# Layer norm's last step moved to ScalarE, middle parts made by a copy, and the attention loop written out

## The chip, the cores and the metric

The kernel runs on one core of a Trainium2 chip. The metric is the time on the device, in microseconds, of one execution. Engines: TensorE (PE; PEld are its weight loads), VectorE (DVE), ScalarE (ACT), GpSimd (POOL), and SyncE (SP), which only issues transfers here.

## The reference, cut to what matters

```python
# x: (32, 256, 128), 16 heads of 8
qkv = (x @ W_qkv.T + b_qkv).reshape(B, T, H, 3 * hs)
q, k, v = qkv[..., :hs], qkv[..., hs:2*hs], qkv[..., 2*hs:]
att = softmax(einsum('bthd,bshd->bhts', q, k) / sqrt(hs))
y = einsum('bhts,bshd->bthd', att, v).reshape(B, T, C) @ W_out.T + b_out
x = layernorm(x + y)                  # (r - mean) / sqrt(var + 1e-5)
# mixture of 8 experts, top 2 by sigmoid scores + bias, and a shared one
out = layernorm(x + shared(x) + sum(score * expert(score * x)))
```

## The kernel before

The work has two stages. **Attention** goes over 32 batches of 256 rows. It is a software pipeline over slots: slot s does a different step for each of nine batches. `Slot` (L165) names them: `load` is batch s+5, `proj` s+4 (keys and queries), `stack` s+3 (values, and the parts loaded back), `maxi` s+2 (scores for the row maxima), `neg` s+1, `soft` s (scores again, exp, values), `tail` s-1 (sums, division), `norm` s-2 (output product, residual, layer norm), `gated` s-3 (gate logits). Slots run from -4 to 34. `slots` (L188) writes out -4 to 2, runs 3 to 26 as a loop of six passes over four slots on each engine, and writes out the rest. In the loop, what a wait compares with depends on the pass and is worked out in registers. **The expert stage** follows: 16 groups of 512 rows, nine experts each, on all engines; its own loop is not touched.

The order within a slot is written out by hand, head by head (h = 0 to 15), with constants that say after which head a small step comes. ScalarE does one exp per head (L565, 128x512, the softmax numerator) and between them `attT`, `v_aug`, `kf`, `qf`, `attc`, `x1T_new` (`ACT_K` = 2 and so on, L174). VectorE does one reduction per head (L1008, the row maximum), and at heads 1, 2, 4: `res` (L1020), its statistics, mean and variance `mv` and `var_eps`. TensorE does four score products a head (L703, L716), the value products (L731), and small products between heads: output and key (L793, L800), values and query (L813, L817), transposes (L833, L849, L865, L871), and the gate (L840). Scores go through three PSUM banks each, so TensorE waits for the exp or the reduction of two to four heads ago. All these are in-order queues.

GpSimd (L430) does per slot: the maxima in two parts (L441, L443), `x_bo` (L457), and queries and keys split into three bf16 parts. For keys: part 0 is `kf` rounded (L463), `rk` = kf - part 0 (L465), part 1 = kf - part 0 rounded (L476), part 2 = rk - part 1 (L484); the same for queries (L485 to L490). Between them come the power that gives `rstd` (L470), two TENSOR_SCALAR that make `x1_new` from `res` (L479), and last the copy of `x1T_new` (L499). SP stores the parts to DRAM when they are done, loads them back as stacks a slot later, and stores `x1_new` (L363). TensorE transposes `x1_new` after heads 12 and 13 (L865).

In the last slots no batch is left to project, later none to take maxima of, and VectorE does the routing of the first 6144 rows between the statistics and `var_eps` of slots 30 and 31 (L959 to L976).

Of the kernel before, what the change touches and what calls it, by code (L numbers as in the profile page):

```python
# [14 lines left out]
P = 128  # L15
# [34 lines left out]
def attention_moe_layer(nc, x, xT, wqT, wkT, wvT, bq, bk, bv, woT, bo, gateT, ebias, rank, w1T, w3T, w2T, out):  # L50
# [19 lines left out]
    with ExitStack() as ctx:  # L70
# [20 lines left out]
        w_hi, w_lo = ([sb(f"{part}_{n}", [P, NE, P], F32R) for n in ("w1", "w3", "w2")] for part in ("hi", "lo"))  # L91
        ident, ident_bf = sb("ident", [P, P]), sb("ident_bf", [P, P], BF16)
        used_first = sb("used_first", [P, P])
        minus_half, ones = sb("minus_half", [P, GT]), sb("ones", [P, NT, 2, PAIRS])

        x1T = sb("x1T", [P, N])
        logits = sb("logits", [P, TILES, E])
# [18 lines left out]
        x_bo = sb("x_bo", [P, NT, C])  # L116
        res = sb("res", [P, NT, C])
        stats, mv = sb("stats", [P, NT, 6]), sb("mv", [P, NT, 2])
        var_eps, rstd = sb("var_eps", [P, NT]), sb("rstd", [P, NT])
        x1_new, x1T_new = sb("x1_new", [P, NT, C]), sb("x1T_new", [P, T])  # L120

        banks = [ctx.enter_context(nc.psum_tensor(f"bank{n}", [P, 512], F32)) for n in range(8)]
# [23 lines left out]
        tok_T, recip_set, att_norm = sem("tok_T"), sem("recip_set"), sem("att_norm")  # L146
        back_T, attc_set = sem("back_T"), sem("attc_set")
        y_mm, xbo_set, res_set = sem("y_mm"), sem("xbo_set"), sem("res_set")
        stats_set, mv_set, eps_set, rstd_set = sem("stats_set"), sem("mv_set"), sem("eps_set"), sem("rstd_set")
        x1_set, x1_kept, x1_T, x1T_set, x1T_kept = (sem(n) for n in ("x1_set", "x1_kept", "x1_T", "x1T_set", "x1T_kept"))  # L150
        gate_mm, logits_set = sem("gate_mm"), sem("logits_set")

# [18 lines left out]

        PE_YK, PE_VQ, PE_TOK, PE_BACK = 0, 2, 4, 6
        DVE_RES, DVE_STATS, DVE_AGGR, DVE_TOK = 1, 2, 4, 9
        ACT_K, ACT_ATT, ACT_V, ACT_Q, ACT_ATTC, ACT_X1T = 2, 4, 5, 6, 13, 14  # L174

# [7 lines left out]
        ACT_ROUTE = 4  # L183
        assert EARLY // NT <= B - 7

        FIRST, LOOPS = 3, (B - 8) // RING

        def slots(engine, body):  # L188

            for s in range(-4, FIRST):  # L190
                body(Slot(0, s))
            with engine.Fori(0, LOOPS) as i:
                for s in range(FIRST, FIRST + RING):
                    body(Slot(i, s))
            for s in range(FIRST + RING * LOOPS, B + 3):
                body(Slot(0, s))


# [213 lines left out]
        def _(pool):  # L412
# [2 lines left out]
            pool.affine_select(out=ident[:], in_=ident[:], compare_op=ALU.not_equal, fill=1.0, base=0,  # L415
                               pattern=[[-1, P]], channel_multiplier=1).then_inc(consts_set, 1)
            pool.memset(minus_half[:], -0.5).then_inc(consts_set, 1)
            pool.memset(ones[:], 1.0).then_inc(consts_set, 1)

            pool.wait_ge(consts_set, 4)  # L420
            pool.tensor_copy(ident_bf[:], ident[:]).then_inc(consts_set, 1)
            columns = ident[:].rearrange("p (g w) -> p g w", w=32)
            pool.tensor_copy(used_first[:, 0:4 * W].rearrange("p (g w) -> p g w", w=W), columns[:, :, 0:W]).then_inc(consts_set, 1)
# [6 lines left out]
            def slot(t):  # L430
# [31 lines left out]
                if p.live:  # L462
                    pool.tensor_copy(k_split[:, 0, :], kf[:]).then_inc(split_step, 1)  # L463
                    pool.wait_ge(split_step, p.count(8, 1))
                    pool.tensor_tensor(rk[:], kf[:], k_split[:, 0, :], ALU.subtract).then_inc(split_step, 1)  # L465
                b = t.norm
                if b.live:

                    pool.wait_ge(eps_set, b.count(1, 1))
                    pool.tensor_tensor(rstd[:], var_eps[:], minus_half[:, 0:NT], ALU.pow).then_inc(rstd_set, 1)  # L470
                    pool.wait_ge(rstd_set, b.count(1, 1))
                    if b.later(1):
                        pool.wait_ge(x1_T, b.count(1, 0))
                        pool.wait_ge(x1_kept, b.count(16, 0))
                if p.live:
                    pool.tensor_tensor(k_split[:, 1, :], kf[:], k_split[:, 0, :], ALU.subtract).then_inc(split_step, 1)  # L476
                if b.live:
                    for i in range(NT):
                        pool.tensor_scalar(x1_new[:, i, :], res[:, i, :], mv[:, i, 0:1], rstd[:, i:i + 1],  # L479
                                           ALU.subtract, ALU.mult).then_inc(x1_set, 1)  # L480
                if p.live:
                    pool.wait_ge(split_step, p.count(8, 3))
                    pool.wait_ge(qk_f, p.count(2, 2))
                    pool.tensor_tensor(k_split[:, 2, :], rk[:], k_split[:, 1, :], ALU.subtract).then_inc(split_step, 1)  # L484
                    pool.tensor_copy(q_split[:, 0, :], qf[:]).then_inc(split_step, 1)  # L485
                    pool.wait_ge(split_step, p.count(8, 5))
                    pool.tensor_tensor(rq[:], qf[:], q_split[:, 0, :], ALU.subtract).then_inc(split_step, 1)
                    pool.tensor_tensor(q_split[:, 1, :], qf[:], q_split[:, 0, :], ALU.subtract).then_inc(split_step, 1)
                    pool.wait_ge(split_step, p.count(8, 7))
                    pool.tensor_tensor(q_split[:, 2, :], rq[:], q_split[:, 1, :], ALU.subtract).then_inc(split_step, 1)  # L490

                    if p.c == RING and not p.looped:

                        for m in range(3):
                            pool.wait_ge(w_hi_set, m + 1)
                            pool.tensor_tensor(w_lo[m][:], w_stage[m], w_hi[m][:], ALU.subtract).then_inc(w_lo_set, 1)
# [39 lines left out]
        def _(act_e):  # L536
# [15 lines left out]
            def slot(t):  # L552
# [6 lines left out]
                for h in range(H):  # L559
# [17 lines left out]
                    if b.live and h == ACT_ATTC:  # L577
# [4 lines left out]
                            act_e.wait_ge(y_mm, b.count(1, 0))  # L582
                        nc.scalar.activation(attc[:], right, ACT.Identity, bias=bv_sb[:, 0:1]).then_inc(attc_set, 1)
                    b = t.norm
                    if b.live and h == ACT_X1T:
                        if t.tail.live:
                            act_e.wait_ge(back_T, t.tail.count(1, 1))
                        else:
                            act_e.wait_ge(x1_T, b.count(1, 1))
                        if b.later(1):  # L590
                            act_e.wait_ge(gate_mm, b.count(1, 0))
                            act_e.wait_ge(x1T_kept, b.count(1, 0))
                        nc.scalar.activation(x1T_new[:], left, ACT.Copy).then_inc(x1T_set, 1)
# [15 lines left out]
                    if b.live and h == ACT_K:  # L609

                        if b.c == 0 and not b.looped:
                            act_e.wait_ge(w_in, 16 * 4)
                            nc.scalar.activation(bqs[:], bq_sb[:], ACT.Copy, scale=SCALE).then_inc(bqs_set, 1)
                            act_e.wait_ge(bqs_set, 1)
                        act_e.wait_ge(k_mm, b.count(1, 1))
                        if t.norm.live:
                            act_e.wait_ge(res_set, t.norm.count(1, 1))
                        if b.later(1):
                            act_e.wait_ge(split_step, b.count(8, -5))
                        nc.scalar.activation(kf[:], right, ACT.Identity, bias=bk_sb[:, 0:1]).then_inc(qk_f, 1)  # L620
                    if b.live and h == ACT_Q:

                        act_e.wait_ge(q_mm, b.count(1, 1))
                        if b.later(1):
                            act_e.wait_ge(split_step, b.count(8, -1))
                        nc.scalar.activation(qf[:], right, ACT.Identity, bias=bqs[:, 0:1], scale=SCALE).then_inc(qk_f, 1)
                        if b.c == 0 and not b.looped:
                            load_constants()
# [64 lines left out]
        def _(pe):  # L693
# [63 lines left out]
            def slot(t):  # L757
# [11 lines left out]
                for p in range(PAIRS):  # L769
# [73 lines left out]
                    if b.live and p == PE_TOK:  # L843

                        pe.wait_ge(max_lo_set, b.count(1, 1))
                        if b.c == 0 and not b.looped:
                            pe.wait_ge(consts_set, 7)
# [363 lines left out]
```

## Time and profile before

| | |
|---|---|
| Median of 3 runs | 840.85 us (838.94 to 841.08) |
| Profiled execution | 841.11 us, span 839.3 us |
| Mean granted TensorE clock | 0.985 of full speed |
| Busy share of the span | TensorE 91%, VectorE 85%, ScalarE 66%, GpSimd 63% |
| Chain that ended last | TensorE 57%, issue 11%, GpSimd 10%, VectorE 9%, DMA 8%, ScalarE 2% |

Times in the rows count from the start of the span. Busy shares over the whole span average stages that have different limits, so the stretches have to be looked at one by one. A stretch of the chain called "issue" is time in which an engine waited for nothing that the profile shows.

### The profile page before, as it was taken

How to read it: one execution, taken by the hardware profiler on the slowest of the kernel's cores; microseconds unless marked ns; L12 is line 12 of the kernel's file. 1: busy time of each engine (PE TensorE's matmuls, PEld its weight loads, DVE VectorE, ACT ScalarE, POOL GpSimd, SP SyncE). 2: the span in 40 equal slices, each digit the busy share in tenths (PEclk: the TensorE clock that was granted, in tenths of full speed). 3: DMA queues.
4: the chain of work that ended last, by engine and by line, in shares of the span. 5: the costliest groups of instructions: out<-in, count | busy, mean ns of one | idle time of the engine just before them, and what ended most of it. 6: DMA issues, size and time to landing. Idle time of an engine off the chain costs nothing.

```text
span 839.3 us, 21651 instructions
## 1 busy us (share of the span) xinstructions
PE 761.5 (91%) x6228; PEld 471.5 (56%) x6228; DVE 709.6 (85%) x1430; ACT 557.7 (66%) x1128; POOL 528.8 (63%) x686
## 2 busy tenths in 40 slices
PE   1698999999999999999996889999999999999994
PEld 0244555555555555555544666666666666666662
DVE  5577999999999999999984788888888788888885
ACT  1147888888888888888884566655555655665651
POOL 3446766766766776676434466667666766676664
PEclk9998999999999999999999899999999999999997
DMA  5643656565565656555412724334343444444440
GB/s 157 167 118 106 169 170 169 141 186 152 159 162 168 156 149 181 153 149 163 114 35 75 180 80 109 103 102 108 103 120 110 125 125 125 125 125 124 113 90 25
DMA packets 201642, 108.83 MB, mean 130 GB/s; under 512 B 10496, under 2 KB 201088, under 8 KB 201600
## 3 DMA queue, kind: packets, MB, share of 16 engines
q1 hardware_dynamic: 200048, 105.88, 47.1%
q10 hardware_dynamic: 1552, 2.44, 1.0%
q8 instruction: 20, 0.33, 0.2%
q14 instruction: 22, 0.18, 0.1%
HBM read 73.94 MB, written 33.82 MB: 128 GB/s over the span
## 4 chain that ended last, share of the span: by engine, by line
PE 57%; issue 11%; POOL 10%; DVE 9%; DMA 8%; ACT 2%; SPq 1%; DVEq 1%; POOLq 0%; ACTq 0%
PE bank L731 14%; PE bank L703 10%; PE bank L716 7%; DMA probs<-route_dram 6%; POOL place L517 3%; PE bank L738 3%; DVE k_stack L1082 3%; PE bank L739 3%; PE bank L740 3%; PE bank L813 2%; POOL rstd L526 2%; PE bank L896 2%; PE bank L793 2%; PE bank L800 2%; PE bank L833 2%
## 5 line engine op out<-in xcount | busy, mean ns | idle before, releaser
L1008 DVE TENSOR_REDUCE negmax<-bank 128x2 f32<-128x512 f32 x512 | 321.0, 680 | 33.6 <-PE bank L716 28.0
L565 ACT ACTIVATE probs<-bank 128x512 f32<-128x512 f32 x512 | 292.0, 605 | 63.1 <-PE bank L703 60.0
L716 PE MATMUL bank<-k_stack,q_stack 48*128 48x256 bf16 x1024 | 163.1, 284 | 9.4 <-DMA k_stack<-k_parts_dram 5.3
L703 PE MATMUL bank<-q_stack,k_stack 50*128 50x256 bf16 x1024 | 159.1, 276 | 4.0 <-ACT probs L565 3.5
L738 PE MATMUL bank<-x_hi,hi_w 128*128 128x512 f32 x288 | 137.6, 478 | 11.3 <-DVE k_stack L1082 8.1
L731 PE MATMUL bank<-probs,v_aug 128*32 128x256 f32 x2048 | 138.5, 388 | 0.4 <-ACT attT L576 0.4
L703 PEld LDWEIGHTS bank<-q_stack,k_stack 50*128 50x128 bf16 x1024 | 76.6, 95 | 88.4 <-ACT probs L565 49.5
L1072 DVE TENSOR_TENSOR k_stack<-bank,probs 128x512 f32<-128x512 f32 x128 | 87.8, 686 | 44.3 <-DMA probs<-route_dram 28.0
L739 PE MATMUL bank<-x_hi,lo_w 128*128 128x512 f32 x288 | 114.8, 398 | 0.0
L740 PE MATMUL bank<-x_lo,hi_w 128*128 128x512 f32 x288 | 114.6, 398 | 0.0
L517 POOL TENSOR_TENSOR k_stack<-k_stack,probs 128x512 f32<-128x512 f32 x48 | 62.2, 1296 | 80.1 <-DVE k_stack L1082 72.3
L675 ACT ACTIVATE q_stack<-k_stack 128x512 f32<-128x512 f32 x128 | 79.6, 622 | 36.7 <-DVE k_stack L1072 36.4
L653 ACT ACTIVATE probs<-probs 128x512 f32<-128x512 f32 x128 | 79.5, 621 | 12.3 <-DMA probs<-route_dram 10.9
L716 PEld LDWEIGHTS bank<-k_stack,q_stack 48*128 48x128 bf16 x1024 | 72.0, 96 | 27.0 <-DVE negmax L1008 11.6
L738 PEld LDWEIGHTS bank<-x_hi,hi_w 128*128 128x128 f32 x288 | 54.7, 190 | 51.4 <-DVE k_stack L1082 19.1
L731 PEld LDWEIGHTS bank<-probs,v_aug 128*32 128x32 f32 x2048 | 53.9, 110 | 50.2 <-issue 19.9
L662 ACT ACTIVATE hs_hi<-k_stack 128x512 fp32r<-128x512 f32 x48 | 30.2, 628 | 57.9 <-POOL k_stack L517 57.9
L517 POOL TENSOR_TENSOR k_stack<-q_stack,probs 128x512 f32<-128x512 f32 x32 | 41.3, 1292 | 39.2 <-DVE q_stack L1082 29.2
L739 PEld LDWEIGHTS bank<-x_hi,lo_w 128*128 128x128 f32 x288 | 54.9, 191 | 19.0 <-issue 10.2
L1082 DVE TENSOR_TENSOR k_stack<-bank,q_stack 128x512 f32<-128x512 f32 x96 | 64.0, 679 | 0.7 <-ACT q_stack L675 0.7
L517 POOL TENSOR_TENSOR place<-k_stack,probs 128x512 f32<-128x512 f32 x48 | 61.8, 1287 | 1.4 <-ACT hs_hi L662 0.9
L740 PEld LDWEIGHTS bank<-x_lo,hi_w 128*128 128x128 f32 x288 | 54.7, 190 | 13.3
(113 smaller groups left out, 1323.8 us busy)
## 6 DMA issues: line engine op xcount, KB each, us to landing
probs<-route_dram SPq DMA_DIRECT2D x128, 256.0 KB, 5.8
q_stack<-q_parts_dram SPq DMA_DIRECT2D x64, 192.0 KB, 3.2
k_stack<-k_parts_dram SPq DMA_DIRECT2D x64, 192.0 KB, 4.0
k_parts_dram<-k_parts SPq DMA_DIRECT2D x32, 192.0 KB, 2.0
q_parts_dram<-q_parts SPq DMA_DIRECT2D x32, 192.0 KB, 2.0
xT_sb<-xT SPq DMA_DIRECT2D x32, 128.0 KB, 2.1
k_parts_dram<-k_parts SPq DMA_DIRECT2D x32, 128.0 KB, 1.9
q_parts_dram<-q_parts SPq DMA_DIRECT2D x32, 128.0 KB, 2.0
```

What stands on the lines that cost most here:

```text
L517: pool.tensor_tensor(hid_s[n % DEPTH], hid[n % DEPTH], weight2_b[n - 1], ALU.mult).then_inc(hids_set, 1)
L565: nc.scalar.activation(probs[h][:], score_ps[EXP_BANK[h]][:].rearrange("p (j t) -> p j t", j=NT), ACT.Exp).then_inc(exp_done, 1)
L675: nc.scalar.activation(act[n % DEPTH], gated[n % DEPTH] if n else up1_ps[0][:], ACT.Silu).then_inc(act_set, 1)
L703: mm = pe.matmul(score_ps[EXP_BANK[h]][:, j * T:(j + 1) * T], k_stack[b.ring][first:last, h // 2, j * P:(j + 1) * P], q_stack[b.ring][firs ...
L716: mm = pe.matmul(max_ps[MAX_BANK[h]][:, i * T:(i + 1) * T], q_stack[b.ring][first:last, h // 2, i * P:(i + 1) * P], k_stack[b.ring][first: ...
L731: mm = pe.matmul(av_ps[32 * hh:32 * hh + 32, half * T:(half + 1) * T], v_aug[b.ring][:, 2 * j + half, u, hh, :], probs[4 * quad + hh][:, j ...
L738: pe.matmul(ps[:], w_hi[m][:, n, :], hi[:], start=start, stop=False)
L739: pe.matmul(ps[:], w_lo[m][:, n, :], hi[:], start=False, stop=False)
L740: return pe.matmul(ps[:], w_hi[m][:, n, :], lo[:], start=False, stop=stop)
L1008: nc.vector.tensor_reduce(negmax[b.ring % 2][:, :, column], max_ps[MAX_BANK[h]][:].rearrange("p (i s) -> p i s", i=NT), AX_X, ALU.max, neg ...
L1072: nc.vector.tensor_tensor(gated[n % DEPTH], up1_ps[n % DEPTH][:], weight_b[e], ALU.mult).then_inc(gated_set, 1)
L1082: nc.vector.tensor_tensor(hid[n % DEPTH], up3_ps[n % DEPTH][:], act[n % DEPTH], ALU.mult).then_inc(hid_set, 1)
```

## The change

Three edits. (1) Layer norm's last step: GpSimd no longer does (res - mean) x rstd; it makes `shift` = -mean x rstd in two products on 128x2, and ScalarE does Identity(res x rstd + shift), two ACTIVATEs behind the exp of head 9. The waits for the previous `x1_new` to be transposed and stored move with them to ScalarE; GpSimd waits for the previous `x1_set` before the power. (2) The middle part of keys and queries is `rk` or `rq` rounded, a copy that waits for it, in place of a subtraction; the keys' one stands before the power, and `kf` and `qf` are free one step earlier. (3) `slots` has no loop: all 39 slots are written out.

```diff
+        minus_half, ones, minus_one = ..., sb("minus_one", [P, NT])
+        ACT_K, ACT_ATT, ACT_V, ACT_Q, ACT_NORM, ACT_ATTC, ACT_X1T = 2, 4, 5, 6, 9, 13, 14
...
-            for s in range(-4, FIRST):
-                body(Slot(0, s))
-            with engine.Fori(0, LOOPS) as i:
-                for s in range(FIRST, FIRST + RING):
-                    body(Slot(i, s))
-            for s in range(FIRST + RING * LOOPS, B + 3):
+            for s in range(-4, B + 3):
                 body(Slot(0, s))
...
+            pool.memset(minus_one[:], -1.0).then_inc(consts_set, 1)
...
+                    pool.wait_ge(split_step, p.count(8, 2))
+                    pool.tensor_copy(k_split[:, 1, :], rk[:]).then_inc(split_step, 1)
                 b = t.norm
                 if b.live:
                     pool.wait_ge(eps_set, b.count(1, 1))
+                    if b.later(1):
+                        pool.wait_ge(x1_set, b.count(2, 0))
                     pool.tensor_tensor(rstd[:], var_eps[:], minus_half[:, 0:NT], ALU.pow).then_inc(rstd_set, 1)
+                    pool.tensor_tensor(shift[:], mv[:, :, 0], minus_one[:], ALU.mult).then_inc(shift_step, 1)
                     pool.wait_ge(rstd_set, b.count(1, 1))
-                    if b.later(1):
-                        pool.wait_ge(x1_T, b.count(1, 0))
-                        pool.wait_ge(x1_kept, b.count(16, 0))
-                if p.live:
-                    pool.tensor_tensor(k_split[:, 1, :], kf[:], k_split[:, 0, :], ALU.subtract).then_inc(split_step, 1)
-                if b.live:
-                    for i in range(NT):
-                        pool.tensor_scalar(x1_new[:, i, :], res[:, i, :], mv[:, i, 0:1], rstd[:, i:i + 1],
-                                           ALU.subtract, ALU.mult).then_inc(x1_set, 1)
+                    pool.wait_ge(shift_step, b.count(2, 1))
+                    pool.tensor_tensor(shift[:], shift[:], rstd[:], ALU.mult).then_inc(shift_step, 1)
...
-                    pool.tensor_tensor(q_split[:, 1, :], qf[:], q_split[:, 0, :], ALU.subtract).then_inc(split_step, 1)
+                    pool.wait_ge(split_step, p.count(8, 6))
+                    pool.tensor_copy(q_split[:, 1, :], rq[:]).then_inc(split_step, 1)
...
+                    if b.live and h == ACT_NORM:
+                        act_e.wait_ge(shift_step, b.count(2, 2))
+                        if b.later(1):
+                            act_e.wait_ge(x1_T, b.count(1, 0))
+                            act_e.wait_ge(x1_kept, b.count(16, 0))
+                        for i in range(NT):
+                            nc.scalar.activation(x1_new[:, i, :], res[:, i, :], ACT.Identity, bias=shift[:, i:i + 1],
+                                                 scale=rstd[:, i:i + 1]).then_inc(x1_set, 1)
```

## Rows read from the trace of the kernel before

**Rows 1.** Busy by stretch: loop slots, drain. Engine's busy us (instructions), clock, DMA share, GB/s

```profile
core 0: us, PE busy (x) PEld busy (x) DVE busy (x) ACT busy (x) POOL busy (x), PEclk, DMA share, GB/s
94.00:389.90 295.90, 295.90 (x3704) 171.73 (x3696) 285.15 (x625) 253.97 (x553) 204.79 (x360) 1.00 0.60 161
425.00:464.40 39.40, 28.97 (x312) 17.12 (x307) 22.30 (x57) 23.40 (x49) 15.51 (x23) 0.98 0.28 79
```

**Rows 2.** Groups by line, 100 to 400 us: busy us, mean ns, idle before

```profile
L565 ACT ACTIVATE probs<-bank 128x512 f32<-128x512 f32 x390 | 224.2, 606 | 42.4 <-PE bank L703 40.3
...
L479 POOL TENSOR_SCALAR x_new<-res,mv,rstd 128x128 f32<-128x128 f32 x50 | 39.6, 798 | 0.0
...
L484 POOL TENSOR_TENSOR k_parts<-rk,k_parts 128x256 bf16<-128x256 f32 x25 | 16.8, 674 | 0.0
...
L583 ACT ACTIVATE attc<-bank,bv_sb 128x256 f32<-128x256 f32 x24 | 11.5, 479 | 0.0
...
L605 ACT ACTIVATE v_aug<-bank 128x128 f32<-128x128 f32 x48 | 11.2, 302 | 0.0
...
L463 POOL CAST k_parts<-kf 128x256 bf16<-128x256 f32 x24 | 9.6, 398 | 0.0
...
L441 POOL TENSOR_TENSOR max_two<-negmax,ones 128x32 bf16<-128x32 f32 x24 | 6.1, 253 | 1.0 <-DVE negmax L1008 0.9
```

**Rows 3.** One slot in order of time: start, duration, instructions, idle before

```profile
247.64 0.72 POOL L470 TENSOR_TENSOR rstd<-var_eps,minus_half 128x2 f32<-128x2 f32 x1 [0.27 <-DVE var_eps L1030]
...
250.97 1.09 ACT L565 ACTIVATE probs<-bank 128x512 f32<-128x512 f32 x2 [0.63 <-PE bank L703]
...
252.08 0.09 PEld L703 LDWEIGHTS bank<-q_stack,k_stack 50*128 50x128 bf16 x1 [0.41 <-ACT probs L565]
```

**Rows 4.** Busy by stretch: first pass, second pass, one slot inside a pass

```profile
95.27:144.91 49.64, 49.64 (x619) 28.70 (x617) 47.60 (x105) 42.41 (x94) 34.14 (x61) 1.00 0.60 162
144.91:194.21 49.30, 49.30 (x619) 28.60 (x618) 47.53 (x105) 42.34 (x94) 34.08 (x61) 1.00 0.59 160
354.40:366.68 12.28, 12.28 (x157) 7.14 (x155) 11.82 (x28) 10.58 (x25) 8.52 (x15) 1.00 0.59 163
```

**Rows 5.** First batch: GpSimd in order of time, and the chain

```profile
7.87 0.67 POOL L476 TENSOR_TENSOR k_parts<-kf,k_parts 128x256 bf16<-128x256 f32 x1
8.63 0.67 POOL L484 TENSOR_TENSOR k_parts<-rk,k_parts 128x256 bf16<-128x256 f32 x1
...
13.74 8.49 DMA q_parts_dram<-q_parts
```

**Rows 6.** VectorE around res: slot 8, in the loop; slot 27, outside it

```profile
157.98 0.42 DVE L1020 TENSOR_TENSOR res<-bank,x_bo 128x256 f32<-128x256 f32 x1
158.66 0.69 DVE L1008 TENSOR_REDUCE negmax<-bank 128x2 f32<-128x512 f32 x1 [0.25 <-PE bank L716]
...
391.88 0.42 DVE L1020 TENSOR_TENSOR res<-bank,x_bo 128x256 f32<-128x256 f32 x1
392.34 0.69 DVE L1008 TENSOR_REDUCE negmax<-bank 128x2 f32<-128x512 f32 x1
```

**Rows 7.** A queue of instruction loads: packets, MB, share of 16 engines

```profile
q8 instruction: 20, 0.33, 0.2%
```

**Rows 8.** The drain: order of time, and ScalarE's busy time after head 10

```profile
432.70 0.72 POOL L470 TENSOR_TENSOR rstd<-var_eps,minus_half 128x2 f32<-128x2 f32 x1 [3.96 <-DVE var_eps L1030]
...
433.32 1.09 ACT L565 ACTIVATE probs<-bank 128x512 f32<-128x512 f32 x2 [0.39 <-PE bank L703]
...
443.51 0.72 POOL L470 TENSOR_TENSOR rstd<-var_eps,minus_half 128x2 f32<-128x2 f32 x1 [3.93 <-DVE var_eps L1030]
...
462.03 0.41 PE L865 MATMUL bank<-ident,x_new 128*128 128x128 f32 x2 [2.96 <-POOL x_new L479]
...
433.32:443.89 10.57, 9.28 (x116) 4.76 (x120) 8.62 (x22) 9.53 (x19) 3.19 (x6) 1.00 0.14 40
443.89:448.22 4.33, 3.08 (x44) 1.39 (x44) 1.63 (x5) 3.29 (x8) 2.30 (x3) 1.00 0.11 32
```

**Rows 9.** Busy by stretch: the start of the expert stage

```profile
463.00:469.80 6.80, 6.33 (x16) 4.76 (x17) 3.67 (x7) 4.91 (x9) 1.60 (x2) 0.50 0.60 175
```

More of the change, by code:

```diff
@@ L93, in attention_moe_layer @@
         used_first = sb("used_first", [P, P])
-        minus_half, ones = sb("minus_half", [P, GT]), sb("ones", [P, NT, 2, PAIRS])
+        minus_half, ones, minus_one = sb("minus_half", [P, GT]), sb("ones", [P, NT, 2, PAIRS]), sb("minus_one", [P, NT])
         x1T = sb("x1T", [P, N])
@@ L118, in attention_moe_layer @@
         stats, mv = sb("stats", [P, NT, 6]), sb("mv", [P, NT, 2])
-        var_eps, rstd = sb("var_eps", [P, NT]), sb("rstd", [P, NT])
+        var_eps, rstd, shift = sb("var_eps", [P, NT]), sb("rstd", [P, NT]), sb("shift", [P, NT])
         x1_new, x1T_new = sb("x1_new", [P, NT, C]), sb("x1T_new", [P, T])
@@ L148, in attention_moe_layer @@
         y_mm, xbo_set, res_set = sem("y_mm"), sem("xbo_set"), sem("res_set")
-        stats_set, mv_set, eps_set, rstd_set = sem("stats_set"), sem("mv_set"), sem("eps_set"), sem("rstd_set")
+        stats_set, mv_set, eps_set, rstd_set, shift_step = (sem(n) for n in ("stats_set", "mv_set", "eps_set", "rstd_set", "shift_step"))
         x1_set, x1_kept, x1_T, x1T_set, x1T_kept = (sem(n) for n in ("x1_set", "x1_kept", "x1_T", "x1T_set", "x1T_kept"))
@@ L173, in attention_moe_layer @@
         DVE_RES, DVE_STATS, DVE_AGGR, DVE_TOK = 1, 2, 4, 9
-        ACT_K, ACT_ATT, ACT_V, ACT_Q, ACT_ATTC, ACT_X1T = 2, 4, 5, 6, 13, 14
+        ACT_K, ACT_ATT, ACT_V, ACT_Q, ACT_NORM, ACT_ATTC, ACT_X1T = 2, 4, 5, 6, 9, 13, 14
         CHUNK = P // E
@@ L184, in attention_moe_layer @@
         assert EARLY // NT <= B - 7
-        FIRST, LOOPS = 3, (B - 8) // RING
         def slots(engine, body):
-            for s in range(-4, FIRST):
-                body(Slot(0, s))
-            with engine.Fori(0, LOOPS) as i:
-                for s in range(FIRST, FIRST + RING):
-                    body(Slot(i, s))
-            for s in range(FIRST + RING * LOOPS, B + 3):
+            for s in range(-4, B + 3):
                 body(Slot(0, s))
@@ L417, in _ @@
             pool.memset(minus_half[:], -0.5).then_inc(consts_set, 1)
+            pool.memset(minus_one[:], -1.0).then_inc(consts_set, 1)
             pool.memset(ones[:], 1.0).then_inc(consts_set, 1)
-            pool.wait_ge(consts_set, 4)
+            pool.wait_ge(consts_set, 5)
             pool.tensor_copy(ident_bf[:], ident[:]).then_inc(consts_set, 1)
@@ L618, in slot @@
                         if b.later(1):
-                            act_e.wait_ge(split_step, b.count(8, -5))
+                            act_e.wait_ge(split_step, b.count(8, -6))
                         nc.scalar.activation(kf[:], right, ACT.Identity, bias=bk_sb[:, 0:1]).then_inc(qk_f, 1)
@@ L624, in slot @@
                         if b.later(1):
-                            act_e.wait_ge(split_step, b.count(8, -1))
+                            act_e.wait_ge(split_step, b.count(8, -2))
                         nc.scalar.activation(qf[:], right, ACT.Identity, bias=bqs[:, 0:1], scale=SCALE).then_inc(qk_f, 1)
@@ L846, in slot @@
                         if b.c == 0 and not b.looped:
-                            pe.wait_ge(consts_set, 7)
+                            pe.wait_ge(consts_set, 8)
                         for i in range(NT):
```

## The prediction

> **What bounds the kernel now.** I read the busy table by stage first. Attention for 24 of its slots (one slot advances every pipeline stage by one batch) runs from 94 to 390 us, and TensorE's matmul engine is busy in all 295.90 us of it, at full clock; VectorE follows with 285, ScalarE has 254 and GpSimd 205 [rows 1]. The reader is to see two things: TensorE sets the pace, and VectorE is only 4% behind it. ScalarE and GpSimd, the two engines whose work is changed, have 42 and 91 us of idle time there. From 425 to 464 us the pipeline drains; there TensorE is busy in only 29 of 39 us, so other engines matter.
>
> Then the groups of instructions for the prices [rows 2], and the order of time within one slot for what is late when [rows 3]. Last, the busy table cut at the same matmul (L800) of each pass through the four-slot loop [rows 4]: the first pass takes 49.64 us, the next 49.30, and a slot away from the jump back 12.28.
>
> **The norm moved to ScalarE.** Removed per batch: two TENSOR_SCALAR of 798 ns on GpSimd, 1.6 us. Added on GpSimd: two products on 128x2. The trace has none; the nearest rows are a 128x32 product at 253 ns [rows 2] and, of the same shape but with a power, 0.72 us [rows 3]. I take 0.25 each, with 0.1 between the second product and what it waits for; the floor is nothing and the ceiling 0.72. Added on ScalarE: two 128x128 ACTIVATEs with scale and bias by pointer. A 128x128 one without takes 302 ns, a 128x256 one with a bias 479 ns [rows 2]. Half the columns make it cheaper, a second pointer dearer, so I take the upper one, 0.48. Successive ACTIVATEs overlap: two exps of 606 ns [rows 2] take 1.09 us together [rows 3], 0.12 less than their sum. So a pair holds ScalarE for 2 x 0.36 = 0.72 us and its second result is there at 0.84. Bounds: 0.5 and 1.0.
>
> The Trainium skill (ScalarE: Activation LUTs, What ACT_TABLE_LOAD costs) gives 186 ns plus 0.833 per column, 93 more for each pointer and 93 of overlap; by it one takes 479 ns and a pair holds the engine for 0.77. No row shows two pointers; the sum would be the same.
>
> Does the pair fit? It comes after the exp of head 9. ScalarE then idles 0.63 us before head 10's, so the pair pushes that exp by about 0.1. Behind it in ScalarE's queue wait the exps of heads 10 to 15, attc and x1T_new; TensorE waits for them. Its next score product after head 10's exp (which ends near 251.57, half of the x2 row) starts at 252.08 [rows 3], so 0.5 us more is covered, by matmuls that keep TensorE busy. The pair would have to hold ScalarE for over 1.1 us to cost anything. Are the products in time? The power starts at 247.64 [rows 3]; shift is ready 0.72 + 0.25 + 0.1 + 0.25 = 1.32 later, at 248.96, or 249.3 with the copy that now stands before the power. ScalarE asks at 250.34. The transpose of x1 on TensorE and the store of x1 on SP's queue come later than 251. Steady state: 0. Without the cover, 0.7 us for each of 28 slots.
>
> **The middle parts.** Two subtractions (674 ns) become copies (398 ns) [rows 2], but each copy now waits for the remainder, a gap of about 0.09 (the third part starts that much behind the second's end now [rows 5]). GpSimd gets 0.55 - 0.2 back per batch, and with the 1.6 it has some 1.4 us more idle time. It is not late anywhere in steady state: all it does is hidden under TensorE. Its parts are stored and loaded back by SP, whose stores stand behind other DMAs of the queue; so no transfer moves much. In the first batch they are on the path: the middle part starts at 7.87, right behind the remainder, and the third at 8.63 [rows 5]. A copy that starts at 8.0, after the remainder's end and the gap, ends at 8.4, and the third part starts near 8.5, 0.14 earlier; the same for the queries, 0.28 in all. The landing of those parts takes 8.49 us and is next on the chain [rows 5]; if it isn't queue-bound the gain stays. I take -0.3, bounds 0 and -0.4. One more memset on GpSimd at 1.4 us lies in its idle time before the first key: 0.
>
> **The loop written out.** Twenty more slots of code run straight. Removed: six returns or exits and the register arithmetic ahead of waits. From the pass after the first, a pass is 49.30 against 4 x 12.28 = 49.12 [rows 4]. Six passes: 5 x 0.18 + (49.64 - 49.12) = 1.4 us, the most there is while TensorE's own matmuls take 12.27. VectorE gains too: after res the next reduction starts 0.68 us later inside the loop and 0.46 outside it [rows 6], so it gets 0.2 us of slack a slot, which is where TensorE's small waits in the loop came from. Against it: instructions must now be loaded all along. The queue of instruction loads moved 20 packets [rows 7]; two or three times that is under 1 MB against 108. The first pass, whose code had to be loaded, is 0.34 slower than the second. I take it that most of that is covered by the new slack: -1.2, bounds -1.4 and 5 x 0.34 = +1.7.
>
> The Trainium skill (Runtime: NRT & Kernel Launch, Instruction fetch mechanics) says that code is fetched ahead in blocks, a crossing mostly hidden, and that a taken branch can force a wait. The first pass fits a small cost of crossing, the later ones a small cost of the branch. By "hidden" the term would be -1.4.
>
> **The drain.** Here the order matters. In the slots where VectorE also does routing, var_eps is late: the power starts at 432.70 and the exp of head 10 at 433.32 [rows 8]. After the change ScalarE stands before the pair until 432.70 + 1.32 = 434.02, and head 10 starts at 434.74, 1.4 us later. Up to the same exp of the next slot ScalarE has 10.57 - 9.53 = 1.04 us of idle time to catch up [rows 8]: +0.4. The next slot has the same, with a power at 443.51 + 0.4: ready 445.23, head 10 at 445.95 instead of 443.89 (where the second stretch begins), 2.06 less the 4.33 - 3.29 = 1.04 idle after it [rows 8], so +1.0 in all. The last two norms have no exps, and TensorE stands waiting for them, 2.96 us at the last [rows 8]. From the power's start GpSimd took 0.72 + 0.1 + 2 x 0.80 = 2.4; now 1.32 + 0.1 + 0.84 = 2.26, or 1.6 with both lower bounds. I take -0.3 each. Drain: +0.4, bounds -1.0 and +2.0.
>
> **Sum.** The profiled execution took 841.11 us (the median of the runs is 840.85). -1.2 - 0.3 + 0.4 = -1.1: 840.0. Nothing in the expert stage changes, 375 us of it.
>
> **Rivals.**
> A, cold code: straight code keeps the first pass's pace, 49.64. For: that pass. Against: VectorE's waits there have register work before them, and straight code has none. Loop term +1.7: 842.9. Chance 0.13.
> B, the clock: right after the drain the granted clock is half for 6.8 us, with 6.33 us of matmuls [rows 9], after TensorE's idle stretches. If shorter waits keep the clock up, those take half: -3.2, 836.8. Against: the waits shrink by tenths only. Chance 0.10.
> C, slower: a small product on GpSimd costs as the power does, 0.72, the only row of that shape. Shift is ready at 2.26, still before 250.34 in steady state, but in the drain ScalarE stands longer: 2.4 - 1.04 = +1.3, then 3.9 - 1.04 = +2.9, then twice +0.8: +4.5 instead of +0.4, giving 844.1. It decides from a ready time near 2.0 us behind the power. Against: the 128x32 product takes 0.25, so the power itself is what costs. Chance 0.08.
> D, a pair of 0.8 each, as on GpSimd: 1.6 held, 0.5 over the 1.1 covered, x 28 = +14, 854. Against: no ACTIVATE row of this size is near. Chance 0.03.
> E, nothing of the loop is saved and the drain balances: 841, inside the first case's spread; chance 0.10.
> The forecast itself has 0.56.
>
> **Numbers.** 0.3% is 2.5 us, about what a measurement of this kernel tells from no change. The forecast's terms reach from -1.4 - 0.4 - 1.0 = -2.8 to +1.7 + 2.0 = +3.7. Faster: B and a small part of the forecast and of a drain that gains, 0.21. Slower: C, D and the top of A, 0.14. Same: 0.65. Range 837.2 to 843.2: it leaves out C, D and most of B.
>
> **What would show it.** After: a slot every 12.27 us with no pauses every fourth; ScalarE's idle before head 10's exp gone, TensorE still busy throughout; GpSimd's busy time down by some 45 us; the reduction 0.46 after res in every slot; instruction packets two to three times as many; the exp of head 10 late by 1.4 and 2 us in the two routing slots. Wrong if VectorE or ScalarE opens gaps on TensorE in each slot, if instruction loads cost more than 0.1 us a slot, or if the expert stage shifts against its transfers.

## The result and the profile after

| | before | after | ratio, 95% interval |
|---|---|---|---|
| median of 10 runs each | 840.97 us | 843.01 us (840.54 to 847.30) | 1.0039 [1.0021, 1.0057] |
| profiled execution | 841.11 us, span 839.3 | 847.30 us, span 845.5 | |

The change makes the kernel 0.4% slower. The forecast was 840.0 us; the median lies inside the range and on the other side of no change. The profiled execution is the longest of the ten, so stages are compared over several kernels below.

The first table again is busy time by stretch, of the changed kernel, columns as in [rows 1]:

```profile
94.00:389.90 295.90, 295.90 (x3705) 170.80 (x3704) 289.25 (x626) 269.83 (x602) 162.40 (x360) 1.00 0.70 163
```

TensorE is still busy in all of the stretch. GpSimd lost 42 us of work and ScalarE gained 16, as meant. One number moved that no step of the change touches: the DMA engines' share, 0.60 in [rows 1], is 0.70 for the same bytes (161 and 163 GB/s).

Queues (packets, MB, share of 16 engines) and issues (KB each, median us to landing), from the page of the kernel before:

```profile
q1 hardware_dynamic: 200048, 105.88, 47.1%
...
q_stack<-q_parts_dram SPq DMA_DIRECT2D x64, 192.0 KB, 3.2
k_stack<-k_parts_dram SPq DMA_DIRECT2D x64, 192.0 KB, 4.0
```

and of the changed kernel:

```profile
q1 hardware_dynamic: 200048, 105.88, 51.7%
...
q8 instruction: 45, 0.74, 0.4%
...
q_stack<-q_parts_dram SPq DMA_DIRECT2D x64, 192.0 KB, 3.7
k_stack<-k_parts_dram SPq DMA_DIRECT2D x64, 192.0 KB, 4.9
```

The same packets and the same bytes take a tenth more of the DMA engines' time. The loads that bring the parts back as stacks land 0.5 and 0.9 us later. Instruction loads went from 20 packets [rows 7] to 45, still under 1 MB.

Passes in the changed kernel, cut at the same matmul (L801) as in [rows 4], which now has no jump behind it; the last row is one slot:

```profile
96.64:145.83 49.19, 49.19 (x618) 28.44 (x617) 48.15 (x106) 44.89 (x101) 27.08 (x60) 1.00 0.70 166
145.83:195.03 49.20, 49.20 (x618) 28.41 (x617) 48.15 (x106) 44.88 (x101) 27.07 (x60) 1.00 0.69 156
355.10:367.40 12.30, 12.30 (x156) 7.12 (x155) 11.85 (x28) 11.22 (x26) 6.76 (x15) 1.00 0.72 163
```

One slot in order of time (start, duration), the rows that answer to [rows 3]:

```profile
248.80 0.71 POOL L468 TENSOR_TENSOR rstd<-var_eps,minus_half 128x2 f32<-128x2 f32 x1
...
249.49 0.20 POOL L469 TENSOR_TENSOR shift<-mv,minus_one 128x2 f32<-128x2 f32 x1
...
249.82 0.19 POOL L472 TENSOR_TENSOR shift<-shift,rstd 128x2 f32<-128x2 f32 x1
...
251.06 0.87 ACT L584 ACTIVATE x_new<-res,shift,rstd 128x128 f32<-128x128 f32 x2
```

The shift is ready at 250.01 and ScalarE takes it at 251.06, when it gets there: no wait.

The first batch: the two middle parts (L461, L481) and the last part on GpSimd, then pieces of the chain, to be held against [rows 5]:

```profile
7.98 0.40 POOL L461 CAST k_parts<-rk 128x256 bf16<-128x256 f32 x1
...
10.45 0.40 POOL L481 CAST q_parts<-rq 128x256 bf16<-128x256 f32 x1
10.93 0.67 POOL L483 TENSOR_TENSOR q_parts<-rq,q_parts 128x256 bf16<-128x256 f32 x1
...
12.99 9.39 DMA q_parts_dram<-q_parts
...
23.80 5.12 DMA k_stack<-k_parts_dram
...
29.06 0.61 PE bank L717 x4
```

and the same end of the chain in the kernel before:

```profile
23.64 4.12 DMA k_stack<-k_parts_dram
...
27.90 0.61 PE bank L716 x4
```

The parts are issued 0.75 us earlier (12.99 against 13.74) and land within 0.2 of when they did (22.38 against 22.23): the landing takes 9.39 in place of 8.49. Then the first load of `k_stack` takes 1.0 longer, and the first row-maxima product starts 1.16 later.

In slot 28, the first without a batch to project, TensorE has a pause that the kernel before has not. SP's queue there, before:

```profile
401.23 1.46 SPq L371 DMA_DIRECT2D k_parts_dram<-k_parts  x3
...
406.55 0.84 SPq L339 DMA_DIRECT2D q_stack<-q_parts_dram  x2
407.43 0.99 SPq L339 DMA_DIRECT2D k_stack<-k_parts_dram  x2
410.85 1.28 SPq L345 DMA_DIRECT2D q_stack<-max_rows  x2
```

and after, with the pause of TensorE in the last row (in brackets: idle before it, and what ended that):

```profile
401.95 3.34 SPq L364 DMA_DIRECT2D k_parts_dram<-k_parts  x3
...
408.78 0.84 SPq L332 DMA_DIRECT2D q_stack<-q_parts_dram  x2
409.67 0.99 SPq L332 DMA_DIRECT2D k_stack<-k_parts_dram  x2
411.63 1.26 SPq L338 DMA_DIRECT2D q_stack<-max_rows  x2
...
415.98 0.28 PE L704 MATMUL bank<-q_stack,k_stack 50*128 50x256 bf16 x1 [0.73 <-DMA q_stack<-max_rows]
```

The stores' issue takes 3.34 in place of 1.46, the stacks' loads start over 2 us later, and the 8 KB of row maxima that go out behind them come late to TensorE. The longer issue alone doesn't make the pause: `after_256_bytes`, a run shown below that has none, takes 2.71 for it.

The drain, the rows that answer to [rows 8]:

```profile
434.51 0.71 POOL L468 TENSOR_TENSOR rstd<-var_eps,minus_half 128x2 f32<-128x2 f32 x1 [3.96 <-DVE var_eps L1031]
...
435.77 0.88 ACT L584 ACTIVATE x_new<-res,shift,rstd 128x128 f32<-128x128 f32 x2 [1.02 <-POOL shift L472]
436.55 2.14 ACT L558 ACTIVATE probs<-bank 128x512 f32<-128x512 f32 x4
...
467.10 0.41 PE L866 MATMUL bank<-ident,x_new 128*128 128x128 f32 x2 [2.81 <-ACT x_new L584]
```

In slot 30 the exp of head 10 (436.55) comes 2.04 after the power's start, exactly as worked out; slot 31, where it comes later, is looked at below. The last wait for `x_new` is 2.81 in place of 2.96.

### The profile page after: what moved, and what is told of

It is laid out like the page before. It is cut to its first block, busy times and chain, and to the rows that moved or that the text cites. A ratio compares the mean times of both kernels' runs of the same rounds, so it can differ in the third digit from the quotient of the medians.

```text
span 845.5 us, 19602 instructions
## 1 busy us (share of the span) xinstructions
PE 762.4 (90%) x6228; PEld 472.6 (56%) x6228; DVE 708.3 (84%) x1430; ACT 579.6 (69%) x1192; POOL 472.3 (56%) x687
## 3 DMA queue, kind: packets, MB, share of 16 engines
q10 hardware_dynamic: 1552, 2.44, 1.0%
## 4 chain that ended last, share of the span: by engine, by line
PE 60%; DVE 11%; POOL 9%; issue 8%; DMA 7%; ACT 2%; SPq 1%; DVEq 1%; POOLq 0%; ACTq 0%
PE bank L732 15%; PE bank L704 10%; PE bank L717 7%; DMA probs<-route_dram 5%; PE bank L739 4%; PE bank L741 3%; PE bank L740 3%; DVE k_stack L1083 3%; POOL place L510 3%; POOL rstd L519 3%; PE bank L814 2%; PE bank L897 2%; PE bank L794 2%; PE bank L834 2%; PE bank L801 2%
## 5 line engine op out<-in xcount | busy, mean ns | idle before, releaser
L717 PE MATMUL bank<-k_stack,q_stack 48*128 48x256 bf16 x1024 | 164.2, 284 | 11.4 <-DMA k_stack<-k_parts_dram 7.3
L717 PEld LDWEIGHTS bank<-k_stack,q_stack 48*128 48x128 bf16 x1024 | 71.8, 96 | 29.9 <-issue 11.8
L492 POOL COPY x1T<-x1T_new 128x256 f32<-128x256 f32 x32 | 12.7, 396 | 93.6 <-ACT x1T_new L594 93.6
```

The lines of the kernel that those rows point to most:

```text
L717: mm = pe.matmul(max_ps[MAX_BANK[h]][:, i * T:(i + 1) * T], q_stack[b.ring][first:last, h // 2, i * P:(i + 1) * P], k_stack[b.ring][first: ...
```

## The experiments

All kernels compute the whole result. Ratios are to the kernel before, timed on the same chip.

**Parts of the change alone.** Four theories stood: the norm on ScalarE costs in the drain; straight code costs; the parts' stores, issued earlier, collide with loads; or something that comes with the new tiles slows the transfers. `straight_only` is edit (3), `straight_copy` edits (3) and (2), `norm_only` edit (1) with the loop kept, `after_again` the whole change.

```diff
# straight_only
-            with engine.Fori(0, LOOPS) as i:
-                for s in range(FIRST, FIRST + RING):
-                    body(Slot(i, s))
...
+            for s in range(-4, B + 3):
# straight_copy: that, and
-                    pool.tensor_tensor(k_split[:, 1, :], kf[:], k_split[:, 0, :], ALU.subtract)
+                    pool.tensor_copy(k_split[:, 1, :], rk[:])
# norm_only: the kernel before, and
+                        for i in range(NT):
+                            nc.scalar.activation(x1_new[:, i, :], res[:, i, :], ACT.Identity, ...)
```

> The loop written out and nothing else. Theory D (drain: the change loses its time in the last slots, where ScalarE stands waiting for shift with exps behind it, and TensorE's pauses lower its clock): nothing of that is here, so this run is faster than before by 0.6 to 1.2 us (839.8 to 840.4), TensorE's key product comes every 12.27 to 12.30 us. Theory C (cold code: instruction loads slow the transfers and the engines, so that the stacks land late): slower than before by 1 to 2 us, with the first stack's landing 1 us later and a hole of 1 us before slot 29.

> The loop written out and the middle parts as copies, the norm still on GpSimd. Theory D: as straight_only, at most 0.3 us faster. Theory C: as straight_only, slower than before by 1 to 2 us. Third possibility, E (earlier stores: the queries' parts of the second batch are stored 0.9 us earlier and meet the load of the first stack): the first scores 1 us later than with the subtractions, so 1 us slower than straight_only.

> The norm on ScalarE and nothing else; loop and subtractions as before. Theory D: slower than before by 2.5 to 4 us (843.5 to 845), all of it from slot 30 on: the x1 transposes of slots 30 to 33 come 0.7, 2.1, 3.4 us later and more than before. Theory C: no difference from before (841).

> The changed kernel unchanged, for a second profile and for times in the same job. Both theories: 2 us slower than before (843), between 1 and 4. Theory D: slots 30 to 33 take at least 2 us more than before in this profile too, and the difference in them holds when the expert stage differs. Theory C: the hole before slot 29 and the late first stack are there again.

Measured: 0.9997 [0.9979, 1.0015]; 1.0000 [0.9979, 1.0020]; 1.0050 [1.0027, 1.0074]; 1.0043 [1.0025, 1.0061]. Straight code and copies change nothing that can be told; whatever costs comes with the norm. But the share of q1 is 46.8 and 47.0% in the first two and 52.1 and 51.5% in the last two, and no step of the norm touches those transfers. What `norm_only` shares with the whole change, besides the step itself, is two new tiles of 8 bytes.

**The tiles' places.** The addresses that the build assigns show what they do: every tile starts at a multiple of 32 bytes, and `minus_one` lies ahead of `x1T`, so `x1T` and the tiles behind it move by 32 (by 64 behind `shift`). `q_stack` starts at 89344 = 349 x 256 in the kernel before and at 89376 in the changed one. `before_8_bytes` is the kernel before with an unused tile in that place. `after_tiles_last` is the changed kernel with its two tiles behind all others.

```diff
# before_8_bytes
-        minus_half, ones = sb("minus_half", [P, GT]), sb("ones", [P, NT, 2, PAIRS])
+        minus_half, ones, unused = ..., sb("unused", [P, NT])
# after_tiles_last, behind the last tile of all
+        minus_one, shift = sb("minus_one", [P, NT]), sb("shift", [P, NT])
# drain_on_gpsimd: that, and for the last four batches
+                        for i in range(NT):
+                            pool.tensor_scalar(x1_new[:, i, :], res[:, i, :], mv[:, i, 0:1], rstd[:, i:i + 1], ...)
# drain_gp_shifted: the same norms, the tiles where the change puts them
```

> The kernel before with one unused 8-byte tile declared where the change declares minus_one, so that every tile behind it lies 8 bytes further on. Theory A (addresses: the new tile moved all later tiles off the places that suited the transfers, so 512-byte packets take longer): the packets' share of the DMA engines rises from 47% to about 52%, k_stack lands in 4.9 instead of 4.0 us, the first row-maxima product comes 0.6 to 1.2 us later, and the time is 0.5 to 2 us longer. Theory D alone (the drain is all of the loss): nothing changes, neither the share nor the time.

> The changed kernel with minus_one and shift declared behind all other tiles, so that the others lie where they lay before. Theory A with D: share back at 47%, no hole of 0.7 to 1 us before slot 29, first scores 0.6 to 1.2 us earlier, time 1 to 2 us less than the changed kernel (842 to 843); slots 30 to 33 still 2 us longer than before. Theory D alone: as the changed kernel, 843.5 to 844.

> after_tiles_last, but the last four batches' norm (slots 30 to 33) is done on GpSimd as before. Theories A and D together: the drain from slot 27 to the last transpose of x1 is back at 71.4 us, the clock falls once there as before, and the time is 839.5 to 840.5, at or 0.5 us below before. Had something else caused the loss (ScalarE's pair in every slot, the straight code), it stays at 842 or more.

> The changed kernel with its tiles where it has them, and the last four norms on GpSimd. Theory A with D: share 52%, a hole before slot 29, time 0.5 to 2 us more than drain_on_gpsimd (840.5 to 842). Theory D alone: equal to drain_on_gpsimd.

Measured: 1.0030 [1.0005, 1.0055]; 0.9990 [0.9970, 1.0011]; 1.0005 [0.9983, 1.0028]; 1.0037 [1.0018, 1.0056]. Eight unused bytes cost about as much as the change, and for the change without the move no cost can be told. Giving GpSimd the drain back helps in neither place. The theory of the drain falls, and with it my first reading of `norm_only`. The kernel before with eight unused bytes, the stretch of [rows 1] and its page:

```profile
94.00:389.90 295.90, 294.70 (x3680) 171.07 (x3682) 283.94 (x623) 252.97 (x551) 203.19 (x359) 1.00 0.70 161
```

```profile
q1 hardware_dynamic: 200048, 105.88, 52.2%
```

Share 0.70 again, with every instruction as before, and here TensorE loses 1.2 us in the stretch.

**Which step of address.** The unused tile made 64, 128 and 256 bytes; `two_on_gpsimd` is `after_tiles_last` with only the norms of slots 30 and 31 on GpSimd.

```diff
# before_64_bytes, before_128_bytes, before_256_bytes
+        ..., sb("unused", [P, 16])   # 32, 64
# stacks_moved, only_stacks_off, around q_stack and k_stack
+        unused = sb("unused", [P, 8])
...
+        unused2 = sb("unused2", [P, 8])   # only_stacks_off: 56
# others_moved, ahead of x1T and of q_stack; all_but_stacks: 8, 56 and 8 behind k_stack
+        unused = sb("unused", [P, 8])
```

> The kernel before with an unused tile of 64 bytes (not 8) ahead of x1T, so that every later tile moves but still starts on a multiple of 64 bytes. Theory A64 (what counts is whether a tile starts on a multiple of 64 bytes or lies 32 past one): share of the DMA engines 47%, k_stack lands in 4.0 us, time as before, 840 to 841. Theory A-any (any move off the old places costs, 256 or 512 bytes being what counts): share 52%, 1 to 3 us slower.

> The kernel before with 32 unused bytes ahead of q_stack and 32 behind k_stack, so that only the eight stacks lie 32 bytes past a multiple of 64. Theory S (the loads of the stacks, in 512-byte packets, are what the address slows): share 50 to 52%, k_stack lands in 4.9 us, first row-maxima product 0.6 us or more later, 1 to 3 us slower than before. Rival O (the parts, probs and other tiles count): share 47 to 48%, time as before.

> The kernel before with every tile behind ones 32 bytes past a multiple of 64 except the eight stacks, which lie on one. Theory S: share 47 to 48%, k_stack lands in 4.0 to 4.2 us, time as before (840 to 841.5). Rival O: share 50 to 52%, 1 to 3 us slower.

> after_tiles_last with the norm of the two slots that also route (30 and 31) on GpSimd, all others on ScalarE. Meant as the best of both: straight code saves 0.6 us, slots 30 and 31 take 22.0 us as before instead of 23.3, slots 32 and 33 keep the 0.3 to 0.5 us that ScalarE saves. Sum -1 us: 839.5, which can't be told from before by the time, only by the stages in the profile. If the time is over 841, the granted clock of the drain decides more than these terms.

Measured: 1.0023 [1.0003, 1.0043]; 1.0015 [0.9995, 1.0035]; 1.0027 [1.0003, 1.0051]; 0.9990 [0.9971, 1.0010]. A multiple of 64 doesn't suffice, as I had expected it to: share 50.9%. `stacks_moved` and `others_moved` leave the stacks 32 and 64 bytes past a multiple of 256 both, with shares of 52.8 and 50.8%, so they couldn't tell which tiles count; that was badly designed. For the transfers the next four can. `two_on_gpsimd`, meant as the best of both, is no faster than `after_tiles_last`.

> The same with an unused tile of 128 bytes: later tiles start 128 bytes past a multiple of 256. Nothing is left out of the computation. Theory A256: share of q1 50 to 52%, k_stack 4.7 to 4.9 us, ratio 1.002 to 1.004. Rival A128 (multiples of 128 suffice): share 47%, k_stack 4.0, ratio 0.999 to 1.001.

> The kernel before with an unused tile of 256 bytes where minus_one stands in the changed kernel, so every later tile lies 256 bytes further and starts again at a multiple of 256 bytes. Nothing is left out of the computation. Theory A256 (what counts is whether a tile starts at a multiple of 256 bytes): queue q1 busy 47% as before, k_stack lands in 4.0 to 4.1 us, ratio 0.998 to 1.001 to the kernel before. Rival (only the old places, or multiples of 512, are quick): share 50 to 52%, ratio 1.002 to 1.005.

> The kernel before with 32 unused bytes ahead of q_stack and 224 behind k_stack, so only the stacks start off a multiple of 256 bytes. Nothing is left out of the computation. Theory S (the loads of the stacks carry the cost): share of q1 50 to 52%, k_stack 4.7 to 5.1 us, ratio 1.002 to 1.004. Rival O (the other tiles carry it): 47 to 48%, k_stack 4.0 to 4.2, ratio 0.999 to 1.001.

> The reverse: 32 unused bytes ahead of x1T, 224 ahead of q_stack and 32 behind k_stack, so the stacks start at multiples of 256 bytes and the other tiles 32 bytes past them. Nothing is left out of the computation. Theory S: share of q1 47 to 48%, k_stack 4.0 to 4.2 us, ratio 0.999 to 1.001. Rival O: share 50 to 52%, ratio 1.002 to 1.004.

Measured: 0.9997 [0.9974, 1.0020]; 0.9986 [0.9963, 1.0009]; 1.0007 [0.9983, 1.0032]; 0.9987 [0.9964, 1.0010]. `before_128_bytes`:

```profile
q1 hardware_dynamic: 200048, 105.88, 50.6%
...
k_stack<-k_parts_dram SPq DMA_DIRECT2D x64, 192.0 KB, 4.5
```

`before_256_bytes`:

```profile
q1 hardware_dynamic: 200048, 105.88, 47.1%
...
k_stack<-k_parts_dram SPq DMA_DIRECT2D x64, 192.0 KB, 4.0
```

`only_stacks_off`:

```profile
q1 hardware_dynamic: 200048, 105.88, 51.2%
...
k_stack<-k_parts_dram SPq DMA_DIRECT2D x64, 192.0 KB, 5.0
```

`all_but_stacks`:

```profile
q1 hardware_dynamic: 200048, 105.88, 47.3%
...
k_stack<-k_parts_dram SPq DMA_DIRECT2D x64, 192.0 KB, 4.0
```

For the transfers this is plain: starts at multiples of 256 bytes are quick wherever they lie, 128 past one is not, and of all tiles it is the stacks that count. For the time it is not: all four intervals hold 1, and the expected +0.2 to +0.4% of the two off their place didn't show. Of the six forms of the kernel before with the stacks off a multiple of 256, three have intervals above 1 (`before_8_bytes`, `before_64_bytes`, `others_moved`), and the six ratios go from 0.9997 to 1.0030. `only_stacks_off` (1.0007) and `before_8_bytes` (1.0030) have the stacks at the same address, and their intervals overlap. So the slower loads are shown to depend on the stacks' place; that the stacks alone carry the time, and not also the other moved tiles, is not shown.

**The changed kernel both ways, on one chip.** `after_256_bytes` is the changed kernel with 224 unused bytes behind `minus_one`; the other is the changed kernel as it is.

```diff
-        minus_half, ones, minus_one = ..., sb("minus_one", [P, NT])
+        minus_half, ones, minus_one, _ = ..., sb("minus_one", [P, NT]), sb("unused", [P, 56])
```

> The changed kernel with 224 unused bytes behind minus_one, so the big tiles behind it start at multiples of 256 bytes again, elsewhere than in either kernel. Nothing is left out of the computation. Theory: packets as in the kernel before (q1 47%, k_stack 4.0 to 4.1 us), first row-maxima product at 27.0 to 27.9 us, ratio 0.997 to 1.001, and at least 0.003 below the next run. Rival (the rest of the change costs the time and the places only part of it): packets the same, ratio 1.002 or more.

> The changed kernel unaltered, on the same chip as the run above: q1 51 to 52%, k_stack 4.9 us, first row-maxima product at 28.3 to 29.1 us, ratio 1.003 to 1.006.

Measured: 0.9969 [0.9952, 0.9986], median 838.96 us of 12; and 1.0046 [1.0029, 1.0064], median 844.61 of 11. 5.6 us lie between two kernels that differ in unused bytes alone. Part of it goes with TensorE's clock: the mean granted clock was 0.984 or less in 8 of the 11 executions of `after_once_more`, in 1 of the 12 of `after_256_bytes`, and in 10 of 22 of the kernel before beside them. The executions above 0.984 alone have medians of 841.48 us (3 executions), 838.96 (11) and 840.12 (12): between the two forms 2.5 us are left. `after_256_bytes` in the stretch of [rows 1], and its page:

```profile
94.00:389.90 295.90, 295.90 (x3708) 170.93 (x3708) 289.16 (x626) 269.84 (x602) 162.80 (x360) 1.00 0.61 163
```

```profile
q1 hardware_dynamic: 200048, 105.88, 47.4%
```

It is the fastest form of the change. `after_tiles_last`, with the stacks also in their place, gave 0.9990 with an interval that holds 1, so the gain of the change itself is 0.1 to 0.3%, not certainly more than nothing; between the executions above 0.984 it is 1.2 us for `after_256_bytes`.

## Why the prediction was wrong

Stage by stage, each the time between the starts of two matmuls (us): the first row-maxima product (L716, L717); from the key product of slot 2 to the output product (L793, L794) of slot 27; between successive output products; and 15 groups of the expert stage, from the first transpose of one to that of the last (L906, L907; the line differs from kernel to kernel).

| | row maxima | slots 2-27 | 27-30 | 30 | 31 | 32 | experts | span |
|---|---|---|---|---|---|---|---|---|
| before | 27.90 | 307.41 | 35.99 | 10.79 | 11.24 | 8.62 | 332.57 | 839.3 |
| before_8_bytes | 29.31 | 308.78 | 36.00 | 10.78 | 11.23 | 10.13 | 332.03 | 843.7 |
| straight_only | 27.56 | 306.82 | 36.00 | 10.77 | 11.23 | 8.60 | 332.50 | 835.5 |
| norm_only | 28.53 | 308.24 | 36.00 | 11.46 | 11.88 | 9.89 | 332.71 | 841.0 |
| after | 29.07 | 306.79 | 37.03 | 11.46 | 12.71 | 9.87 | 333.83 | 845.5 |
| after_once_more | 28.37 | 306.80 | 36.68 | 11.46 | 11.87 | 9.89 | 331.43 | 839.7 |
| after_256_bytes | 27.66 | 306.81 | 35.99 | 11.47 | 11.87 | 8.38 | 333.05 | 837.9 |

The table leaves out the stretch from the first row-maxima product to slot 2, which also differs: 55.39, 55.82, 52.49, 53.30, 55.61, 53.91 and 53.40 us, from the top row down. It goes with a stretch of half clock near 67 to 70 us, of 6.8 us in the three longest, 3.4 in the next three and none in `straight_only`. With the stacks in place 4 of 9 profiles have 6.8 us there, with the stacks off 4 of 11, so spans of single profiles differ by up to 3.4 us for a reason that is not the stacks' place.

- **The step that failed** is the price of what the change declares. The prediction has for it "One more memset on GpSimd at 1.4 us lies in its idle time before the first key: 0", and of the transfers it says "so no transfer moves much". The tile that this memset fills moves the tiles behind it, the stacks among them, off a multiple of 256 bytes. Its price is missing from the sum and from every rival. Measured between `after_256_bytes` and `after_once_more` it is 5.6 us, 0.0077 of ratio, of which the clock has a part as said above. That 843.01 lay inside the range was luck: a cost that the sum doesn't hold put it there, and the same kernel's two later medians, 844.12 and 844.61, lie outside.
- **Where it is paid.** The first row-maxima product starts at 27.05 to 27.90 in the nine profiles with the stacks at multiples of 256 (median 27.58), at 27.60 to 29.31 in the eleven without (median 28.53): some 1 us. In straight code slot 28 takes 0.7 to 1.1 more, with the pause shown above. A wait of TensorE's weight loads for the row maxima stands there in ten of the eleven (0.8 to 1.2 us with straight slots, 0.4 to 0.6 each with the loop) and in none of the nine. In the loop form nothing to 1.4 is lost over the slots. The expert stage takes 332.2 to 333.7 with the stacks in place, 331.4 to 336.8 without.
- **The clock's part.** A further 1.5 to 2.6 in slots 31 and 32 comes with half-clock stretches, shown below, in 8 of the 11 profiles with the stacks off their multiple; 2 of the 9 with the stacks in place have one too, for 1.0 and 1.4. Over all executions whose clock is listed, 65 of 126 with the stacks off and 93 of 254 with them in place have a mean granted clock of 0.984 or less. Why the clock falls more often was not settled, and the parts in `after_once_more` don't add up to 5.6, since its profiled execution, at 841.48, was shorter than its median by 3.1.
- **Loop written out:** -0.6 (307.41 to 306.81), predicted -1.2 with -1.4 as the most. The pauses went as said, and a reduction now follows `res` by 0.46 in every slot. The slack was smaller than the prediction read it: 0.68 before [rows 6] is one slot of each pass, and the other three had 0.55. But a straight slot takes 12.30, not the 12.28 that a slot inside a pass took [rows 4], and 25 x 0.02 = 0.5 is most of the missing 0.6; why the slot is longer was not looked for. Cold code (rival A) is ruled out: the first straight pass takes 49.19, against 49.64 in the loop.
- **Copies:** predicted -0.3 if the landing isn't queue-bound. In `after_256_bytes` the landing takes 8.49 from 13.54 and so ends 0.2 earlier than before: -0.2. In the changed kernel it takes 9.39, and nothing is left.
- **Norm, steady state:** 0 as predicted. The pair took 0.87 (0.84), a product on 128x2 0.20 (0.25), the shift was ready 1.21 after the power's start (1.32). Rivals C and D needed 0.72 and 1.6 and are ruled out.
- **Drain:** predicted +0.4 (+0.4, +0.6, -0.3, -0.3). With the clock as before, `after_256_bytes` against before has +0.68, +0.63, -0.24 and, in slot 33, -0.14: +0.9, inside the bounds. The order of events was right, and three sizes were off. In slot 30 head 10's exp is 1.42 late and 0.68 is left, so ScalarE caught up 0.74 of its 1.04. In slot 31 that exp comes 2.44 after the power's start (2.45 in the changed kernel) in place of 2.04, because the second product takes 0.6 there (rows below). And the -0.3 for each of the last two slots has no sum behind it: the prediction's own values, 2.26 against 2.4, make -0.14. The clock (rival B) never stayed up: every profile has 6.8 us or more at half clock behind the drain, as in [rows 9].

Slot 31 of the changed kernel (the power, the second product, VectorE's routing beside it, the pair and the exp of head 10):

```profile
445.97 0.71 POOL L468 TENSOR_TENSOR rstd<-var_eps,minus_half 128x2 f32<-128x2 f32 x1 [3.94 <-DVE var_eps L1031]
...
446.99 0.61 POOL L472 TENSOR_TENSOR shift<-shift,rstd 128x2 f32<-128x2 f32 x1
447.00 0.55 DVE L976 TENSOR_TENSOR q_stack<-q_stack,k_stack 128x384 f32<-128x384 f32 x1
...
447.63 0.88 ACT L584 ACTIVATE x_new<-res,shift,rstd 128x128 f32<-128x128 f32 x2 [1.29 <-POOL shift L472]
448.42 2.14 ACT L558 ACTIVATE probs<-bank 128x512 f32<-128x512 f32 x4
```

In all six profiles that have this product in slot 31 it takes 0.60 to 0.61 there and 0.19 to 0.20 in the other 31 slots. That the VectorE operation beside it is what holds it up is likely and not shown.

The half-clock stretches inside the drain: busy by stretch in the changed kernel, a stretch ahead of the first one and both short ones:

```profile
437.00:450.90 13.90, 11.31 (x132) 5.71 (x136) 8.27 (x20) 12.17 (x27) 2.61 (x5) 1.00 0.14 40
450.90:454.30 3.40, 3.40 (x27) 2.08 (x23) 1.05 (x3) 1.79 (x5) 1.66 (x2) 0.51 0.00 0
457.70:461.10 3.40, 3.33 (x10) 2.85 (x11) 0.02 (x1) 0.75 (x2) 0.40 (x1) 0.50 0.35 77
```

and in the kernel before, over much the same time:

```profile
448.00:455.00 7.00, 4.24 (x46) 3.01 (x39) 3.15 (x10) 2.23 (x6) 4.67 (x6) 1.00 0.12 35
```

The granted clock is 0.51 and 0.50 (1.2 GHz) in the short stretches, with TensorE busy 3.40 and 3.33 of 3.40 us, and 1.00 (2.4 GHz) in the kernel before. Ahead of the first, TensorE had been busy 11.31 of 13.90 us, with its waits for the exps of slot 31.

Without the tile's price the four priced terms (the norm is 0) come to -0.6 - 0.2 + 0.9 = about 0, where I had -1.1. The two kernels that have the whole change with the stacks in place measured -0.8 and -2.6; what lies between about 0 and these is not explained, though beside -2.6 stand the 1 of 12 and 10 of 22 executions at the lower clock.

## What to carry to other kernels

A declared tile is part of a change, even one of eight bytes that nobody reads: look at what lies behind it, and keep tiles that many small packets are loaded into at multiples of 256 bytes, or put new small tiles last. Where the busy share of a queue changes with its packets and bytes the same, compare addresses before any theory of waits. And test a part alone in both places: `norm_only` seemed to convict the norm, and carried the tiles with it.

## What the runs showed of the hardware

- The stacks' loads, among the packets of 512 bytes in q1, tell the place of their target. Over all 512-byte packets of q1 in a profile the mean is 30.8 to 31.8 ns with the stacks at multiples of 256 bytes, 33.8 at 128 past one, 34.0 to 34.1 at 64 past one, and 34.3 to 35.7 at 32 past one; the ninth decile goes from 41 to 51-59 ns. A load of 192 KB into `k_stack` lands in 4.0 to 4.1, 4.5, 4.7 and 4.9 to 5.1 us (medians of a profile). Mean share of the 16 DMA engines over the kernel: 46.8 to 47.9% in place, against 50.6 to 52.8% off it.
- The Trainium skill (DMA: Bandwidth & Descriptors, How a descriptor splits into AXI transactions) says that a descriptor is cut at 256-byte boundaries, and that one which starts off a boundary begins its first transaction at the boundary below. By it, as an estimate, a row of 512 bytes off a boundary touches three pieces in place of two. The section speaks of bytes that are fetched, and here it was the place of the tile written to that changed. The step at 256 agrees with these runs; the rule alone doesn't give the order of 128, 64 and 32, and no run here shows the transactions themselves.
- A product on 128x2 on GpSimd takes 0.19 to 0.20 us where a power of the same shape takes 0.71; beside one VectorE operation on 128x384 it took 0.60 to 0.61.
